# A state-space block with a gated FFN on one core: C spread by transposes of its turned columns, and x1's low half formed on PE and copied by ScalarE

## The reference

```python
def attn(x, W_xproj, W_dt, b_dt, A_log, Dp):
    xz = einsum('btd,pd->btp', x, W_xproj)          # 64 rank + 16 B + 16 C
    dt_raw, Bm, Cm = xz[..., :64], xz[..., 64:80], xz[..., 80:]
    dt = softplus(einsum('btr,dr->btd', dt_raw, W_dt) + b_dt)
    A = -exp(A_log)
    dA, dBx = exp(dt[..., None] * A), dt[..., None] * Bm[:, :, None, :] * x[..., None]
    h_t = dA_t * h_(t-1) + dBx_t ;  y_t = sum_s h_t[:, s] * C_t[s]     # scan over 1024 steps
    return y + Dp * x

def ffn(x, w_gate, w_up, w_down):                    # weights times 1/127
    return (silu(x @ wg.T) * (x @ wu.T)) @ wd.T

x = layernorm(x + attn(x)) ;  x = layernorm(x + ffn(x))
```

## Time and profile before

| | us |
|---|---|
| median of 3 runs | 2120.16 (2118.89 to 2121.01) |
| the profiled execution | 2119.75 |
| its span, first to last instruction | 2118.0 |
| DVE busy in it | 1985.9 (94%) |
| POOL busy | 1926.8 (91%) |
| PE busy | 1558.5 (74%) |
| ACT busy | 1303.6 (62%) |

### The profile page before, as it was taken

The page is one execution under the profiler, slowest core; times in us unless marked ns, Lnnn a source line. Parts: engine busy times, 40 slices in busy tenths (PEclk is TensorE's granted clock), DMA queues, the critical chain, the costliest instruction groups (busy, mean ns, idle before and its releaser), DMA issues.

```text
span 2118.0 us, 30230 instructions
## 1 busy us (share of the span) xinstructions
PE 1558.5 (74%) x8621; PEld 1140.7 (54%) x8744; DVE 1985.9 (94%) x2443; ACT 1303.6 (62%) x2157; POOL 1926.8 (91%) x877
## 2 busy tenths in 40 slices
PE   4677778777778777777777777777777877777775
PEld 1545555455555555555555555555555555555553
DVE  5799999999999999999999999999999999999982
ACT  4566666566666656666666666656666656666442
POOL 6999999999999999999999999999999999999950
PEclk6789999999999999999999999999999999999997
DMA  6332433223433322443322443422443422343200
GB/s 219 111 119 86 141 118 137 102 91 112 140 135 120 117 83 104 140 140 115 125 90 89 140 140 115 140 90 76 138 140 115 140 92 86 126 140 107 79 11 20
DMA packets 93455, 239.90 MB, mean 113 GB/s; under 512 B 8593, under 2 KB 42994, under 8 KB 77042
## 3 DMA queue, kind: packets, MB, share of 16 engines
q1 hardware_dynamic: 93426, 239.55, 32.5%
HBM read 220.65 MB, written 18.87 MB: 113 GB/s over the span
## 4 chain that ended last, share of the span: by engine, by line
issue 30%; POOL 28%; DVE 26%; PE 8%; ACT 6%; DVEq 2%; POOLq 1%; another core or an unknown queue 0%; ACTq 0%
POOL ub L388 16%; DVE h L620 10%; POOL h L398 8%; DVE h L629 6%; PE p_y L807 3%; DVE hid L665 2%; DVE silu_g L659 2%; ACT p_da L490 2%; DVE stats L635 2%; PE p_m L831 2%; DVEq L224 1%; PE p_o L842 1%; PE p_m L821 1%; POOL rstd L405 1%; DVE mean_var L639 1%
## 5 line engine op out<-in xcount | busy, mean ns | idle before, releaser
L388 POOL TENSOR_TENSOR ub<-u,b_bc 128x1024 f32<-128x1024 f32 x512 | 1203.9, 2372 | 0.1
L490 ACT ACTIVATE p_da<-dt,neg_a 128x512 f32<-128x512 f32 x1024 | 697.2, 687 | 426.1 <-DVE h L620 422.0
L620 DVE TENSOR_TENSOR_SCAN h<-p_da,h_carry,ub 128x512 f32<-128x512 f32 x512 | 641.5, 1271 | 2.2 <-ACT p_da L490 0.6
L398 POOL TENSOR_TENSOR h<-h,c_bc 128x1024 f32<-128x1024 f32 x256 | 606.8, 2371 | 33.5 <-ACT h_carry L485 32.8
L620 DVE TENSOR_TENSOR_SCAN h<-p_da,ub 128x512 f32<-128x512 f32 x512 | 610.1, 1212 | 8.1 <-ACT p_da L490 6.4
L807 PE MATMUL p_y<-ident,h 128*128 128x128 f32 x4096 | 572.2, 293 | 60.8 <-POOL h L398 59.6
L807 PEld LDWEIGHTS p_y<-ident,h 128*128 128x128 f32 x4096 | 518.8, 152 | 121.6 <-POOL h L398 81.9
L842 PE MATMUL p_o<-wt_down,hid 128*128 128x256 f32 x1536 | 353.7, 380 | 4.1 <-DVE hid L665 1.8
L842 PEld LDWEIGHTS p_o<-wt_down,hid 128*128 128x128 f32 x1536 | 287.6, 191 | 55.3 <-issue 13.9
L629 DVE TENSOR_TENSOR h<-h,p_c 128x1024 f32<-128x1024 f32 x256 | 306.1, 1196 | 9.8 <-PE p_c L792 5.2
L510 ACT ACTIVATE tanh_g<-p_m 128x512 f32<-128x512 f32 x192 | 114.7, 597 | 263.4 <-PE p_m L831 263.4
(11 more groups left out here) (72 smaller groups left out, 1289.3 us busy)
## 6 DMA issues: line engine op xcount, KB each, us to landing
b_bc<-bc_rows_dram SPq DMA_DIRECT2D x128, 1024.0 KB, 4.7
c_bc<-bc_rows_dram SPq DMA_DIRECT2D x256, 256.0 KB, 6.5
x_in<-in_L_attn_x SPq DMA_DIRECT2D x32, 512.0 KB, 7.2
out_x<-res_n SPq DMA_DIRECT2D x32, 512.0 KB, 3.3
bc_rows_dram<-bc_rows SPq DMA_DIRECT2D x32, 64.0 KB, 2.3
hid<-in_L_ffn_w_gate SPq DMA_DIRECT2D x1, 768.0 KB, 4.9
hid<-in_L_ffn_w_up SPq DMA_DIRECT2D x1, 768.0 KB, 6.7
res<-in_L_ffn_w_down SPq DMA_DIRECT2D x1, 384.0 KB, 7.1
```

Source lines behind the costliest of these rows:

```text
L388: nc.gpsimd.tensor_tensor(ub[:, s % UB_SLOTS, :, :], u[:, par, :, :], b_bc[:, s:s + 1, :].broadcast_to([P, DH, T]), ALU.mult).then_inc(s_u ...
L398: nc.gpsimd.tensor_tensor(h[:, s % H_SLOTS, :, :], h[:, s % H_SLOTS, :, :], c_bc[:, i:i + 1, :].broadcast_to([P, DH, T]), ALU.mult).then_i ...
L490: nc.scalar.activation(p_da[:, q, :], dt[:, par, q, :], ACT.Exp, scale=neg_a[:, q, s:s + 1]).then_inc(s_da, 1)
L620: nc.vector.tensor_tensor_scan(h[:, s % H_SLOTS, q, :], p_da[:, q, :], ub[:, s % UB_SLOTS, q, :], initial, ALU.mult, ALU.add).then_inc(s_s ...
```

## The change

C is no longer split. PE turns the chunk's rows of B and C by four transposes (`bc_turned`) into `p_bc`, which is the PSUM of `p_o`, and ACT copies the 32 columns to `bc_t` (`bc_cols`). For a state of DVE, `broadcast_c` then is four float32 transposes of a column of `bc_t` that is read with stride 0 as 128 equal columns. `rest`, `second_parts`, `third_part`, the copy at L464 and the `selector` are gone, and `project_dt` waits for the plain copies alone; the first `down` of a chunk waits for `bc_cols`.

For x1's low half, PE adds the high half times -1/2048 onto the transposed x1 in `p_m` (`x1_rest`, two float16 products), and ACT copies the result, scaled, as the low half (`x1_low`).

`POOL_STATES` is another set of 8, both lags of the sums are one step longer, and most entries of `AT` move. Waits that were written `wait(engine, ...)` are in places `engine.wait_ge(...)`, which is the same wait.

```diff
-POOL_STATES = (1, 2, 4, 8, 9, 10, 11, 12)
+POOL_STATES = (0, 2, 3, 4, 8, 9, 10, 11)
...
-SUM_LAG = {True: 3, False: 2}
+SUM_LAG = {True: 4, False: 3}
...
-    "dt_of": (4, 2), "u_of": (9, 0),
+    "dt_of": (8, 0), "u_of": (10, 0),
...
-            def bc_out(c, par):
+            def bc_out(c):
...
                 wait(act, s_rows_dram, 16 * c)
-                nc.scalar.copy(bc_rows[FIRST, :], p_m[FIRST, 0, :]).then_inc(s_rows, 1)
-                nc.scalar.copy(bc_parts[BOTH, par, :], p_m[BOTH, 0, :]).then_inc(s_part1, 1)
-
-            def second_parts(c, par):
-                wait(act, s_rest, c + 1)
-                nc.scalar.copy(bc_mid[FIRST, :], bc_rest[FIRST, :]).then_inc(s_part2, 1)
-                nc.scalar.copy(bc_parts[SECOND, par, :], bc_rest[SECOND, :]).then_inc(s_part2, 1)
+                wait(act, s_ones, 3)
+                wait(act, s_bt_ps, c)
+                nc.scalar.copy(bc_rows[ROWS, :], p_m[ROWS, 0, :]).then_inc(s_rows, 1)
+
+            def bc_cols(c, par):
+                act.wait_ge(s_bt_ps, c + 1)
+                wait(act, s_c_ps, ND * (c - 1))
+                nc.scalar.copy(bc_t[:, par, :, :], p_bc[:, :, ROWS]).then_inc(s_bt, 1)
...
+            def x1_low(c):
+                act.wait_ge(s_x1_rest, c + 1)
+                nc.scalar.mul(x1_t[:, 1, :, :], p_m[:, :, :], X1_SCALE).then_inc(s_x1_lo, 1)
...
-            def rest(c, par):
-                wait(dve, s_rank, c + 1)
-                wait(dve, s_part1, c + 1)
-                nc.vector.tensor_tensor(bc_rest[BOTH, :], p_m[BOTH, 0, :], bc_parts[BOTH, par, :],
-                                        ALU.subtract).then_inc(s_rest, 1)
-
-            def third_part(c, par):
-                wait(dve, s_part2, 2 * (c + 1))
-                nc.vector.tensor_tensor(bc_parts[THIRD, par, :], bc_rest[FIRST, :], bc_mid[FIRST, :],
-                                        ALU.subtract).then_inc(s_parts, 1)
...
-            def x1_low(c):
-                wait(dve, s_x1_hi, c + 1)
-                nc.vector.scalar_tensor_tensor(x1_t[:, 1, :, :], p_m[:, :, :], X1_SCALE, x1_t[:, 0, :, :],
-                                               ALU.mult, ALU.subtract).then_inc(s_x1_lo, 1)
...
             def project_dt(c):
-                wait(pe, s_rank, c + 1)
-                wait(pe, s_parts, c + 1)
+                pe.wait_ge(s_rank, c + 1)
+                pe.wait_ge(s_rows, c + 1)
...
             def broadcast_c(c, s, par):
                 i = DVE_STATES.index(s)
-                wait(pe, s_parts, c + 1)
+                pe.wait_ge(s_bt, c + 1)
                 wait(pe, s_hc_dve, ND * c + i)
-                nc.tensor.matmul(p_c[:, 0, :], selector[:, s, :], bc_parts[:, par, :],
-                                 start=True, stop=True).then_inc(s_c_ps, 1)
+                for k in range(TT):
+                    ins = nc.tensor.transpose(p_c[:, 0, k * P:(k + 1) * P],
+                                              bc_t[:, par, k, N + s:N + s + 1].broadcast_to([P, P]), ident[:, :])
+                ins.then_inc(s_c_ps, 1)
+
+            def bc_turned(c):
+                pe.wait_ge(s_rows, c + 1)
+                wait(pe, s_res, 2 * (c - 2))
+                for k in range(TT):
+                    ins = nc.tensor.transpose(p_bc[:, k, :], bc_rows[:, k * P:(k + 1) * P], ident[:, :])
+                ins.then_inc(s_bt_ps, 1)
...
+            def x1_rest(c):
+                pe.wait_ge(s_x1_hi, c + 1)
+                for q in range(DH):
+                    ins = nc.tensor.matmul(p_m[:, q, :], neg_unscale[:, :], x1_t[:, 0, q, :],
+                                           start=False, stop=True, skip_group_check=True)
+                ins.then_inc(s_x1_rest, 1)
...
-            def down(c, k, half):
+            def down(c, k, half, turned):
                 if k == 0 and half == 0:
-                    wait(pe, s_hid, NH * (c + 1))
+                    pe.wait_ge(s_hid, NH * (c + 1))
+                    wait(pe, s_bt, turned)
```

More of the change, by code:

```diff
@@ L35 @@
     "weights": (7, 1),
-    "x_transposed": (0, 0), "x_out": (0, 1), "project": (1, 0), "rank_out": (1, 1), "bc_out": (1, 1), "rest": (2, 1),
-    "second_parts": (2, 0), "third_part": (2, 2), "project_dt": (2, 0), "softplus_abs": (4, 0), "softplus_exp": (4, 0), "softplus_log": (4, 0),
-    "dt_of": (4, 2), "u_of": (9, 0),
-    "z_out": (3, 0), "stats1": (3, 2), "mean1": (4, 0), "norm_inputs": (6, 1), "scalars": (7, 0), "norm1": (7, 0),
-    "x1_transposed": (8, 0), "x1_high": (8, 1), "x1_low": (9, 0),
-    "gate_up": (9, 2), "tanh": (9, 0), "silu": (10, 0), "hidden": (10, 1),
[3 rows of a table removed]
+    "x_transposed": (1, 0), "x_out": (2, 0), "project": (2, 0), "rank_out": (4, 1), "bc_out": (3, 0),
+    "project_dt": (3, 1), "softplus_abs": (5, 0), "softplus_exp": (5, 0), "softplus_log": (7, 0),
+    "dt_of": (8, 0), "u_of": (10, 0),
+    "z_out": (3, 1), "stats1": (4, 1), "mean1": (6, 2), "norm_inputs": (7, 0), "scalars": (5, 1), "norm1": (8, 0),
+    "x1_transposed": (8, 2), "x1_high": (9, 0), "x1_rest": (9, 1), "x1_low": (9, 1),
+    "gate_up": (9, 2), "tanh": (10, 0), "silu": (10, 2), "hidden": (11, 0),
[3 rows of a table added]
+    "bc_turned": (7, 2), "bc_cols": (13, 1),
 }
@@ L674, in residual @@
                     x1[:, 2 * a:2 * a + 2, :], ALU.mult, ALU.add).then_inc(s_res, 1)
-            rest(0, 0)
-            third_part(0, 0)
             dt_of(0, 0)
```

150 lines of the change are left out of this document (72 added, 78 removed), and 6 rows, old and new, of the table AT.

## The result

| | before | after |
|---|---|---|
| median of 20 runs, us | 2119.98 (2118.7 to 2121.98) | 2123.53 (2120.46 to 2127.47) |
| profiled execution: span, us | 2118.0 | 2118.7 |
| mean granted clock of TensorE | 0.928 | 0.957 |

The ratio is 1.0016, with a 95% interval of 1.0009 to 1.0022: if anything slower by a sixth of a per cent, where 2033 was forecast. Of the forecast's 87 us nothing arrived.

A forecast was written before the change was run, and what follows sets the result against it. DVE was taken as the bound, POOL close behind; a chunk falls from 63.14 to 60.3 us. Savings of 82.4 + 4.8 + 3.3 - 3 = 87.5 us gave 2033 us, range 2010 to 2066.

The forecast's parts named there:

- the sum of a chunk: DVE's work plus new idle time makes 60.3 us a chunk against 63.14 before: 2.84 us saved per chunk.
- Rival 4: DVE's saving returns as waits for POOL's B products or a slot of `h`: 2120 us, chance 0.03.
- What leaves DVE: `rest`, `third_part` and `x1_low` leave DVE: its work falls from 61.6 to 59.1 us a chunk.
- The wait for the log: DVE's wait before dt for ACT's log, 1.4 us a chunk, falls to 0 with the log at step 7.
- the pair (a): `silu` and `hidden` side by side on DVE for three tiles: 0.2 us each, 0.6 a chunk, bounds 0 and 1.0.
- The x1 chain (b): Longer chain over PE and ACT to the first tile makes DVE idle 0.3 us a chunk; bounds 0 and 1.5.
- decay (c): DVE's existing waits for `decay`, 7.0 us in all plus small ones, stay at 0.3 us.
- C by four transposes: On PE, four transposes take about 0.5 us where the product took 0.38; DVE's wait for C's row fits.
- Rival 3: PE's clock falls in a chunk's last steps through added transposes, making PE the bound: 2181 us; slower given 0.06.
- Which engine bounds: DVE at 60.3 us a chunk sets the length, POOL just behind at 59.8.
- Rival 1: New idle terms vanish in DVE's slack and POOL's 59.8 us a chunk rules: 2018 us, chance 0.14.
- Start and end: First `project_dt` starts at 14.8 us, 3.3 earlier; later sums and x1's low half add 3 us at the end.

The follow-up runs named there:

- 56 or 115 fills: The kernel before, with 56 or 115 one-column memsets of scratch columns put in front of DVE's program: 2156.92 us with 56, 2233.68 us with 115.
- twelve fills: The changed kernel with twelve one-column memsets of an unused tile added at the start of DVE's program, nothing else changed: 2023.36 us, ratio to before 0.9545.
- the x1 half in the old order: The kernel before with only x1's low half moved to PE and ACT, the rest of the order and C untouched, no memsets: 2118.85 us, ratio 0.9992.

## Why the prediction was wrong, point by point

**The step that failed** is the sum of a chunk, "DVE 59.1 + 0.6 + 0.3 + 0.3 = 60.3 us": it counted what DVE executes and what it waits for on other engines, and had no term for the return of the loop, which cost nothing in the trace of before. The missing term is 13 returns at 7.7 us, 100 us: more than the whole forecast gain. Rival 4 gave the right time (2120) for wrong reasons, waits for `ub` or slots of `h`; no such wait is in the trace. That before's return was free was itself a matter of place: 56 or 115 fills make it cost 37 or 115 us. The term could have been seen ahead: DVE's instructions before and inside the loop can be counted in both programs, and the fetch packets of before show the size of a block. The Trainium skill, Runtime: NRT & Kernel Launch, Instruction fetch mechanics, says that a taken branch to a target outside the window that the instruction memory holds forces a fetch before execution goes on. The traces agree in kind: packets begin at the branch, and DVE stands still. They agree in the whole, 512 instructions on the page and four blocks of 128 here, and differ in the size of a block: the page has two of 256 instructions for an engine like this. By blocks of 256 a loop of 321 touches two or three; the border between 187 and 190 and the packets are those of 128.

**What leaves DVE**: right. Forecast 2.55 us a chunk; busy time fell by 71.4 us over 32 chunks, 2.2, and the dependent pairs put a part back in. With twelve fills DVE is busy 1657.35 / 28 = 59.2 us per 60 us, where 59.1 was forecast.

**The wait for the log**: right, gone. It was oversized: the 44.2 us hold 15.7 us outside the loop, and in the loop's 28 chunks it was 28.5 us, 1.0 a chunk and not 1.4. The sum doesn't rest on it, since it starts from DVE's busy time. The trace of after shows no drain around the table loads either, as in the earlier trace rows; ACT in order of time:

```profile
1002.81 1.28 ACT L473 ACT_TABLE_LOAD   x1
1004.10 1.06 ACT L473 ACTIVATE dt<-dt 128x1024 f32<-128x1024 f32 x1
1005.18 1.28 ACT L482 ACT_TABLE_LOAD   x1
1006.47 1.30 ACT L482 ACTIVATE p_da<-dt,neg_a 128x512 f32<-128x512 f32 x2
```

**New idle time on DVE**: the pair (a) was priced well. In after `silu` and `hid` start 0.77 us apart, against 0.58 for independent neighbours: 0.19, forecast 0.2. In the loop of the kernel with twelve fills that is 8.5 us of gaps and about as much lost overlap, 0.6 us a chunk.

```profile
1017.18 0.66 DVE L642 SCALAR_TENSOR_TENSOR silu_g<-tanh_g,p_m 128x512 f32<-128x512 f32 x1
1017.95 0.69 DVE L648 SCALAR_TENSOR_TENSOR hid<-p_m,silu_g 128x512 f32<-128x512 f32 x1
```

The x1 chain (b) and decay (c) cost less than the 0.6 us taken: in the loop of the kernel with twelve fills DVE's waits for tanh and decay are 2.1 and 1.9 us in all, 0.14 a chunk. That these are small is the new order's doing, as the x1 half in the old order shows.

**C by four transposes**: 0.60 us as against 0.5, and nobody on DVE waits for them in the loop. Rival 3, the low clock in the tiles, is ruled out. This stretch of after, columns as in the earlier trace rows, has a granted clock of 0.98, against 0.99 in the earlier trace rows, with the added transposes in it:

```profile
1010.00:1038.00 28.00, 21.75 (x133) 14.12 (x133) 27.69 (x30) 17.60 (x29) 28.00 (x13) 0.98 0.12 47
```

The clock did fall in after, but behind the stall at the return, not by transposes.

**Which engine bounds**: right, with the stall taken away. The forecast had DVE at 60.3 us a chunk and POOL at 59.8. In the kernel with twelve fills dt's first and last start in the loop give (1862.4 - 178.4) / 28 = 60.14:

```profile
L595 DVE SCALAR_TENSOR_TENSOR dt<-p_m,dt x29: 1207/1209/1216, 178.4 to 1862.4; 128x1024 f32<-128x1024 f32 x29
```

DVE's busy time makes 59.3 of that and its idle time 0.8, where 1.2 was forecast; POOL's work makes 59.8 and its wait for DVE 0.3. Rival 1, POOL's floor, isn't reached: DVE never waits for POOL, though little is left between them. Whether POOL holds DVE back by way of PE's sums, which wait for POOL's products, isn't shown; DVE's waits for PE in the loop are 5.0 us for `down` and 1.2 for up, so it could be little more than that.

**Start and end**: with twelve fills `project_dt` began at 14.99 us, forecast 14.8, but the first dt in the loop's count came 1.0 us later than before, so this wasn't passed on. Of the 95.9 us between the two spans (2118.0 and 2022.1) the 28 chunks between those dt make 83.8. The rest lies from the last dt to the end; since dt itself has moved from step 4 to step 8 of its chunk, these stretches can't be compared piece by piece, and the end's +3 stays unchecked.

Taken together: without the stall the forecast of 2033 would have been 10 us too high, and its range of 2010 to 2066 would have held. In the kernel as it stood, the range missed by 57 us.

## What to carry to other kernels

Before pricing a change to a looped kernel, count each engine's instructions ahead of the loop and in it, and see how many fetch blocks the body touches and how far the return's target stands ahead of the next border; a shift by three instructions can be worth more than the change. When busy time falls and the time doesn't, look at the instruction queues in the list of DMA queues, however small their share, and at what stands at the loop's return. Judge a half of a change only in the order it is meant for: the x1 half was worth 1.8 us (not told from nothing) in one order and 34.6 in another.
